# Two attention sums of a slot moved a step later, with three transposes woven into each

## The reference

```
x = x + layernorm(attention(layernorm(x)))        # rotary q and k, causal softmax, 16 heads, Wo
x = x + layernorm(experts(layernorm(x)))          # 8 low-rank experts (rank 16), softmax router
attention: logits = q k^T / 8, causal;  out = softmax(logits) v;  out @ Wo
```

## Time and profile before

| what | value |
|---|---|
| median of three runs | 1060.23 us (1060.16 to 1060.62) |
| the profiled execution's own time | 1061.01 us |
| its span, first to last instruction | 1059.0 us |
| TensorE (PE) busy | 98% |
| VectorE, ScalarE, GpSimd busy | 71%, 59%, 40% |
| mean granted TensorE clock | 0.998 of 2.4 GHz |

### The profile page before, as it was taken

The page is one execution under the profiler, slowest core; times in us unless marked ns, Lnnn a source line. Parts: engine busy times, 40 slices in busy tenths (PEclk is TensorE's granted clock), DMA queues, the critical chain, the costliest instruction groups (busy, mean ns, idle before and its releaser), DMA issues.

```text
span 1059.0 us, 19431 instructions
## 1 busy us (share of the span) xinstructions
PE 1036.7 (98%) x6135; PEld 896.4 (85%) x6135; DVE 756.4 (71%) x2170; ACT 623.4 (59%) x1454; POOL 419.5 (40%) x422
## 2 busy tenths in 40 slices
PE   7999999999999999999999999999989999999996
PEld 6988888888888888888888888888877888888884
DVE  8576777777776667677766766676666777777777
ACT  7567766767675666567665756666685333333334
POOL 4143515352362445254342625353367232333221
PEclk9999999999999999999999999999999999999999
DMA  7013323331320247011111101110342323332311
GB/s 298 21 65 110 110 70 110 110 110 51 97 87 13 92 161 254 17 51 52 54 51 50 56 11 51 50 52 16 97 163 61 119 82 100 119 105 88 105 61 60
DMA packets 58699, 90.83 MB, mean 86 GB/s; under 512 B 3568, under 2 KB 36336, under 8 KB 58608
## 3 DMA queue, kind: packets, MB, share of 16 engines
q1 hardware_dynamic: 58464, 89.44, 26.1%
q10 hardware_dynamic: 144, 0.26, 0.1%
HBM read 64.52 MB, written 25.17 MB: 85 GB/s over the span
## 4 chain that ended last, share of the span: by engine, by line
PE 78%; DVE 7%; ACT 6%; issue 5%; POOL 1%; DVEq 0%; ACTq 0%; POOLq 0%
PE bank L1525 26%; PE bank L1470 22%; PE bank L1552 14%; PE bank L1584 5%; PE bank L1604 3%; PE bank L1603 2%; PE bank L1722 2%; DVE prob L1123 1%; PE bank L1699 1%; ACT prob L807 1%; ACT pT L818 1%; ACT q_hl L828 1%; PE bank L1723 1%; ACT xin L789 1%; ACT xn L771 1%
## 5 line engine op out<-in xcount | busy, mean ns | idle before, releaser
L653 POOL TENSOR_SCALAR prob<-prob,rinv 128x128 f32<-128x128 f32 (+3 forms) x256 | 137.6, 538 | 433.1 <-DVE rinv L1133 433.1
L807 ACT ACTIVATE prob<-prob,nmax 128x128 f32<-128x128 f32 (+3 forms) x256 | 144.3, 563 | 234.6 <-DVE nmax L1123 232.5
L1525 PE MATMUL bank<-big_hi,w_hi 128*128 128x512 f32 (+1 forms) x520 | 217.2, 418 | 0.3 <-DVE big_lo L1098 0.3
L1525 PE MATMUL bank<-big_hi,w_lo 128*128 128x512 f32 (+1 forms) x520 | 203.3, 391 | 0.0
L1525 PE MATMUL bank<-big_lo,w_hi 128*128 128x512 f32 (+1 forms) x520 | 202.3, 389 | 0.0
L1123 DVE CUSTOM_DVE_ANT_0 prob<-bank,mask 128x256 f32<-128x256 f32 (+2 forms) x192 | 106.3, 554 | 75.6 <-PE bank L1470 75.0
L1552 PE MATMUL bank<-wv_hi,big_hi 128*128 128x256 f32 x512 | 133.0, 294 | 0.0
L1552 PE MATMUL bank<-wv_hi,big_lo 128*128 128x256 f32 x512 | 127.3, 281 | 0.0
L1141 DVE TENSOR_TENSOR pT<-bank,pT 128x128 fp32r<-128x128 f32 (+3 forms) x256 | 124.3, 486 | 1.6 <-ACT pT L818 1.3
L1584 PE MATMUL bank<-ident,prob 128*128 128x128 f32 x640 | 112.1, 273 | 5.6 <-DVE pT L1141 3.0
L1525 PEld LDWEIGHTS bank<-big_hi,w_lo 128*128 128x128 f32 x520 | 97.6, 188 | 21.6
(11 more groups left out here) (159 smaller groups left out, 2279.7 us busy)
## 6 DMA issues: line engine op xcount, KB each, us to landing
w_raw<-in_wqkv SPq DMA_DIRECT2D x32, 512.0 KB, 4.6
wv_raw<-in_wqkv SPq DMA_DIRECT2D x16, 512.0 KB, 4.5
attention_out<-o_sum SPq DMA_DIRECT2D x64, 128.0 KB, 2.3
w_raw<-attention_out SPq DMA_DIRECT2D x16, 512.0 KB, 4.8
land<-in_x SPq DMA_DIRECT2D x16, 512.0 KB, 3.6
out<-res SPq DMA_DIRECT2D x14, 512.0 KB, 2.6
xin<-in_x SPq DMA_DIRECT2D x12, 512.0 KB, 3.7
xT_hold_hi<-xin SPq DMA_DIRECT2D x8, 512.0 KB, 3.6
```

The lines of the kernel that those rows point to most:

```text
L653: pool.tensor_scalar(p, p, rinv[:, q % 4:q % 4 + 1], 1.0, ALU.mult, ALU.mult).then_inc(prob_done, 1)
L807: act.activation(prob[:, q % 4, 0:n], prob[:, q % 4, 0:n], ACT.Exp, scale=-1.0, bias=nmax[:, q % 4:q % 4 + 1], accum_out=rsum[:, q % 4:q % ...
L1525: done = pe.matmul(grp_ps[k][:, cols], w, xt[:, cols], start=at == 0, stop=at == GROUP_MM - 1)
```

## The change

Both sums of a slot go one step later: the first head's to step 1 in every slot, the second head's to step 5 (in slot 33 to step 3, as before). In these two steps the three transposes are no longer between the second and third trio of projection products; they stand inside the sum, each directly ahead of a product with the low part. To have three such places, the first low product is split in two of 256 columns. On ACT `o_lower` of the second head goes from step 5 to step 6, on DVE `o_add` of the second head from step 6 to step 7, and both of the first head to steps 2 and 2. SP's program is not edited.

```diff
-        def first_sum_at(u):
-            return 1 if u % QUAD == QUAD - 1 else 0
+        def sum_steps(u):
+            return 1, 3 if u == UNITS + 1 else 5
...
-                    if s == 1 + first_sum_at(u) and real(u - 2):
+                    if s == 1 + sum_steps(u)[0] and real(u - 2):
                         o_lower(u - 2, 0)
-                    if s == 5 and real(u - 2) and not (isinstance(u, int) and u > UNITS):
+                    if s == 6 and real(u - 2) and not (isinstance(u, int) and u > UNITS):
                         o_lower(u - 2, 1)
...
-                    if s == 1 + first_sum_at(u) and real(u - 2):
+                    if s == 1 + sum_steps(u)[0] and real(u - 2):
                         o_add(u - 2, 0)
-                    if s == 6 and real(u - 2) and not (closing and u > UNITS):
+                    if s == 7 and real(u - 2) and not (closing and u > UNITS):
                         o_add(u - 2, 1)
...
-                    for j in (0, 1, 3, 2):
-                        cols = slice(P * j, SEQ)
-                        if j != 2:
-                            pe.matmul(o_ps[:, cols], v_tile(a, j, h), pT_hi[:, h, j, cols], start=j == 0, stop=False)
-                        pe.matmul(o_ps[0:DH, cols], v_tile(a, j, h)[:, 0:DH], pT_lo[:, h, j, cols], start=False, stop=False)
-                        if j == 2:
-                            last = pe.matmul(o_ps[:, cols], v_tile(a, j, h), pT_hi[:, h, j, cols], start=False, stop=True)
-                    last.then_inc(pv_done, 1)
+                high(0)
+                if blocks:
+                    turn_ready(u, s)
+                turn(0)
+                low(0, 0, SEQ // 2)
+                turn(1)
+                low(0, SEQ // 2, SEQ)
+                high(1)
+                turn(2)
+                low(1, P, SEQ)
+                high(3)
+                low(3, 3 * P, SEQ)
+                low(2, 2 * P, SEQ)
+                high(2).then_inc(pv_done, 1)
...
-                    turn_probs(u, s)
+                    summed = sum_steps(u).index(s) if real(u - 2) and s in sum_steps(u) else None
+                    if summed is None:
+                        turn_probs(u, s)
                     project_next(per * s + 2 * third, per - 2 * third)
-                    if s == first_sum_at(u):
-                        attend(u - 2, b, 0)
-                    if s == (3 if isinstance(u, int) and u == UNITS + 1 else 4):
-                        attend(u - 2, b, 1)
+                    if summed is not None:
+                        attend(u, s, summed)
```

More of the change, by code:

```diff
@@ L1574, in scores @@
                                  ).then_inc(s_done, 1)
-            def turn_probs(u, s):
[L1577 to L1599, removed]
-                    for j in (0, 1, 3, 2):
-                        cols = slice(P * j, SEQ)
-                        if j != 2:
-                            pe.matmul(o_ps[:, cols], v_tile(a, j, h), pT_hi[:, h, j, cols], start=j == 0, stop=False)
-                        pe.matmul(o_ps[0:DH, cols], v_tile(a, j, h)[:, 0:DH], pT_lo[:, h, j, cols], start=False, stop=False)
-                        if j == 2:
-                            last = pe.matmul(o_ps[:, cols], v_tile(a, j, h), pT_hi[:, h, j, cols], start=False, stop=True)
-                    last.then_inc(pv_done, 1)
+            def turned_in(u, s):
+                a, q, g = trailing(u, s, 3)
+                return q % QT + 1 if real(a) else 0
@@ new lines, in turn_ready, with turn_block @@
+            def turn_ready(u, s):
+                a, q, g = trailing(u, s, 3)
+                pe.wait_ge(prob_done, g + 1)
+                if late(g, 2):
+                    pe.wait_ge(pt_hi_done, g - 1)
+                    pe.wait_ge(pt_lo_done, g - 1)
+            def turn_block(u, s, j):
+                q = trailing(u, s, 3)[1]
+                turned = pe.transpose(pt_ps[q % 2][:, P * j:P * j + P], prob[:, q % 4, P * j:P * j + P], ident[:, :])
+                if j == q % QT:
+                    turned.then_inc(t_done, 1)
@@ new lines, in turn_probs, with attend, high, low @@
+            def turn_probs(u, s):
+                if turned_in(u, s):
+                    turn_ready(u, s)
+                for j in range(turned_in(u, s)):
+                    turn_block(u, s, j)
+            def attend(u, s, h):
+                a = u - 2
+                g = STEPS * a + QT * h + QT - 1
+                blocks = turned_in(u, s)
+                pe.wait_ge(pt_hi_done, g + 1)
+                pe.wait_ge(pt_lo_done, g + 1)
+                if h == 0:
+                    m = QUAD * (a // QUAD) + 2 * (a % 2) + 1
+                    pe.wait_ge(v_hi_done, 2 * m + 1 + a % QUAD // 2)
+                    pe.wait_ge(v_lo_done, 2 * m + 1 + a % QUAD // 2)
+                if late(2 * a + h, 1):
+                    pe.wait_ge(osum_done, 2 * a + h)
+                def high(j):
+                    return pe.matmul(o_ps[:, P * j:SEQ], v_tile(a, j, h), pT_hi[:, h, j, P * j:SEQ], start=j == 0, stop=j == 2)
+                def low(j, c0, c1):
+                    pe.matmul(o_ps[0:DH, c0:c1], v_tile(a, j, h)[:, 0:DH], pT_lo[:, h, j, c0:c1], start=False, stop=False)
+                def turn(j):
+                    if j < blocks:
+                        turn_block(u, s, j)
+                high(0)
+                if blocks:
+                    turn_ready(u, s)
+                turn(0)
[9 more added lines that the diff above has]
+                high(2).then_inc(pv_done, 1)
```

## The result

The changed kernel takes **1094.18 us** (median, 1093.17 to 1095.17), the kernel before 1060.42 in the same series: a ratio of **1.0317**, 95% interval 1.0304 to 1.033, so 33.8 us slower. The profiled execution's span is 1093.3 us and its mean granted clock 0.991 (before 1059.0 and 0.998).

The account below looks back on a forecast made before the run. TensorE's own stream was taken to bound the kernel, with only 3.0 us of waits for DVE's low parts. 0.7 + 20 + 4.2 + 3.5 + 3.3 = 31.7 on 1061.0 gave 1092.7, median 0.8 below: 1092 us, range 1069 to 1099.

Parts of the forecast that it names:

- TensorE's own stream: TensorE in all slots: transposes cost the same in their new place, only the split products add time, +0.7 us.
- The first reading: Transposes on TensorE: 0.11 us each is the transpose's own time, and stays so ahead of a low product.
- the step that was built on the rule: Transposes ahead of low products: 0.11 is the next load's time, so the change saves 10.2 us, giving 1084.
- (a): Slots 3 to 9: late staging transfers cost TensorE 2.7 us each, 19 us, with 0.8 for slot 2: +20 us.
- the last link: Slots 3 to 9: VectorE's late low part L1141 holds up TensorE's transposes, 2.7 us lost per slot.
- the slack of 0.3: Slot 5: TensorE has 0.3 us in hand between the low part's end at 161.5 and the transposes at 161.88.
- The other term of the ahead slots: Slots 3 to 9: moving the sum inside a slot was taken to change no amount of TensorE's work.
- (b): Slot 15: SP's reload of the transposed input comes 2.7 us later, TensorE waits 4.4: +4.2 us, at least 2.5.
- (c): Slot 16: reload and projection weights start 4.0 us later, POOL's division holds up the transposes: +3.5 us, at least 3.
- (d): Slot 32: SP requests a Wo tile later, ACT and TensorE wait for it: +3.3 us, between nothing and 3.9.
- The sum: Whole kernel: stream and the four places together add 31.7 us.
- the upper end: Top of the forecast range, with 3 us for the clock not staying at 2.4 GHz through slot 15's wait.

Follow-up runs that it names:

- late-store run: Changed kernel with the second head's store issued one slot later, behind the next slot's loads: 1068.75 us, ratio 1.0079.
- the sooner copy: late-store run with ScalarE's second staging copy ahead of step 3's two q_hl copies in slots that stage: 1059.67 us; in the kernel before, without late store, 1057.61.
- the sooner copy alone: Changed kernel with ScalarE's second staging copy ahead of step 3's two q_hl copies, store left as changed: 1083.55 us, ratio 1.0217.
- the second sum alone: Kernel before with only the second head's sum moved from step 4 to 5, its copy and addition to 6 and 7: 1087.12 us, ratio 1.0243.

## Why the prediction was right, and which steps were off

The time was forecast at 1092.0 and is 1094.2; "slower", with SP's held-back transfers as the cause, was right, and removing SP's wait took 25.4 us away. That the number came out within 2 us is in part luck, as the steps show:

**TensorE's own stream.** The first reading holds, and the steady slots show it best, where nothing waits. Step 3's single transpose of slots 17 and 30, in the kernel before and then in the changed one:

```profile
443.16 0.27 PE L1584 MATMUL bank<-ident,prob 128*128 128x128 f32 x1
...
751.16 0.27 PE L1584 MATMUL bank<-ident,prob 128*128 128x128 f32 x1
```
```profile
475.21 0.27 PE L1590 MATMUL bank<-ident,prob 128*128 128x128 f32 x1
...
783.29 0.27 PE L1590 MATMUL bank<-ident,prob 128*128 128x128 f32 x1
```

The 13 slots between them take 308.00 and 308.08 us. That is 0.08 us for 78 transposes ahead of a low product; at 0.05 less each it would have been 3.9 us the other way. The split was forecast at 0.01 for each sum, 0.26 here. The run with the transposes in a block and no split takes 307.68 for the same slots (474.71 to 782.39), so against that run split and place of the transposes cost 0.4 together. The timeline of slot 6, after, shows the pattern that the earlier trace rows could not:

```profile
180.73 0.27 PE L1590 MATMUL bank<-ident,prob 128*128 128x128 f32 x1
180.75 0.36 PE L1618 MATMUL bank<-pT,v_hl 128*64 128x256 f32 x1
180.95 0.27 PE L1590 MATMUL bank<-ident,prob 128*128 128x128 f32 x1
180.98 0.36 PE L1618 MATMUL bank<-pT,v_hl 128*64 128x256 f32 x1
```

A transpose and a 256-column low product take 0.22 from transpose to transpose, 0.12 less than which is 0.10: nearly the 0.11 of the first reading. The low product's record begins 0.02 to 0.03 behind the transpose and is 0.36 long instead of 0.28, so the cost hides in the record of what follows; only starts two apart tell it. The Trainium skill ("TensorE: Matmul & The Clock Gate", section on LDWEIGHTS) has a load take its number of stationary columns over 1.2 GHz. The records of the loads, after, differ by about that: 188 to 189 ns for the 128 columns of L1525, 135 and 141 for the 64 of L1618, where the rule has 53 between them; a transpose's own load, of 128 columns, is recorded with 141 too, which the rule does not give. What is not borne out is the step that was built on the rule, that a transpose costs what the load behind it takes: with a load of 64 columns behind them these would have been 0.05 shorter.

**(a) Slots 3 to 9.** Forecast 2.7 us each, measured 2.9 in the mean (2.0 to 3.9). SP's delay is nearly as worked out: the addition stands 0.1 behind the reciprocal, 3.7 us later against it than in the earlier trace rows, and in slot 4 the second staging transfer is issued 5.7 us later against the transpose of step 3, 1.7 of them TensorE's own wait in step 5, so 4.0 where 4.4 were forecast. So is the way to ScalarE: 7.4 us from first to second copy were forecast, 7.5 measured. What failed is the last link. I named the transposes of step 6 and their low part L1141. TensorE waits in step 5, at the value products for L1106, 12.4 us in 7 slots, and 4.5 more for L1141 in six of them, but at the single transpose of step 3; at step 6 it doesn't wait. I had taken the slack of 0.3 from the wrong place. I had looked at which of VectorE's instructions follow the copy, and not at which of TensorE's instructions use the bank that the copy empties. With the copy moved sooner L1141 became the wait. Why the size came out right all the same isn't shown. The account has 3.4 us of half clock in these slots, which the sum did not have, and 2.4 us each without them. But the run with the transposes in a block has no half clock there and still loses 2.7 each, 18.8 in all, with longer waits for L1141 (5.9). So the half clock is not the reason, and the match of 2.7 and 2.9 is luck as far as the link is concerned.

**The other term of the ahead slots.** I took the place of the sum on TensorE for free ("Moving it inside a slot changes no amount of TensorE's work"). The amount is the same, the cover isn't: the late-store run shows 6.5 us of waits that stay when SP's wait is gone, with the second sum no longer between the staging transposes and the value products; the sooner copy ends them. I had seen this effect for slot 15's reload in (b) and not for the staging chunk.

**(b) Slot 15.** Forecast +2.7 for the reload and a wait of 4.4; the reload is 2.8 later against the slot (410.02 against the earlier trace rows, less the 21.6 lost until then) and the waits are 0.3 and 3.99. The slot loses 6.8 and not 4.2: the rest is the half clock that begins during that wait, which I had left open. (With the sooner copy alone the stretch in slot 15 is half as long, 3.4 us, and the slot loses 6.1: again less is gained than the account's 1.7.)

**(c) Slot 16.** Forecast 3.5, measured 3.7, but not as told. SP's reload is 3.8 later against the slot (4.0 forecast) and the first weights behind it 4.2, but POOL's addition only 2.8, since these weights took 13.1 us from issue to landing instead of 14.5, a change that the forecast did not have. TensorE waited 1.95, and the half clock behind it costs 1.7 by the account. (The forecast's own sum, 425.0 + 4.0 + 2.0 + 0.7, is 431.7, and 3.3 and not 3.5 later.)

**(d) Slot 32.** Forecast 3.3, measured 2.4. ScalarE does wait 3.05 us for the Wo tile. TensorE's wait of 1.3 for `o_sum` is there as well, and stays with the late store (1.1 of the 2.4), so the tile's share is 1.3.

**The sum.** 31.7 forecast, 34.3 in the span: waits overstated by 5 (31.0 against 25.7), the half clock's 7.8 left out, with 3 us in the upper end for it. The total is nearer than its terms, since the two errors point opposite ways. And 7.8 is the account's figure: by the executions with more clock, an estimate, less than half of it would come off the time.

## What to carry to other kernels

When a block of work moves on an in-order engine, list what it stood between: every pair of instructions of which the later needs a result that the earlier starts (transposes, copy and low part, then products into the same bank) loses that block as cover. When a queue's instruction waits on the moved result, everything behind it in the queue moves too; in this kernel one store made 25 us of it, and putting it a slot later costs nothing. A wait in the list is worth an experiment even in the kernel that seems to have none: a copy of 0.6 us taken ahead of two others gained 2.9 us.

## What the runs showed of the hardware

In the changed kernel the clock fell to 0.5, for 3.4 us behind each of three single waits of TensorE of 1.9 to 2.0 us and for 6.8 us from within one of 4.0, in a kernel whose TensorE is busy otherwise. The length of the wait alone doesn't decide: waits of 1.93 and 1.94 in the same slots of the run with the transposes in a block had no stretch behind them, nor had one of 1.94 in slot 7 of the run with the second sum alone, nor one of 2.2 in slot 31 of the kernel before; what does decide isn't shown. The run with the late store, with waits of 1.6 at most inside the slots, has no such stretch. Counted as work at half speed a stretch costs 1.7 us (2.6 in slot 15) on top of the wait; between the changed kernel and the run without one, slots 3 and 7 differ by 0.8 and 0.5. A product of 256 columns that starts every 0.12 us at full clock started every 0.21 to 0.22 in slot 3:

```profile
110.62 0.36 PE L1552 MATMUL bank<-wv_hi,big_hi 128*128 128x256 f32 x1 [1.97 <-DVE xn L1106]
...
111.05 0.28 PE L1552 MATMUL bank<-wv_hi,big_lo 128*128 128x256 f32 x1
111.17 0.28 PE L1552 MATMUL bank<-wv_hi,big_hi 128*128 128x256 f32 x1
...
111.66 0.42 PE L1552 MATMUL bank<-wv_hi,big_lo 128*128 128x256 f32 x1
111.88 0.42 PE L1552 MATMUL bank<-wv_hi,big_hi 128*128 128x256 f32 x1
```
